# VectorE's operations on neighbouring PSUM banks joined, and a new order of the weights' turning, the scores and the first products of the MLP in a one-core attention and MLP chain

## The chip, the cores and the metric

The kernel runs on one core of a Trainium2 chip. The metric is the time of one execution on the device in microseconds (us). TensorE multiplies matrices and writes the results into PSUM, a memory of eight banks of 128 rows by 512 fp32 columns. VectorE and ScalarE read PSUM; GpSimd works on SBUF alone; SyncE starts DMAs.

## The reference

The input `x` has 4 sequences of 512 tokens with 128 features. Four blocks follow each other, each added to `x` behind a layer norm: attention a (16 heads of width 8), a transformer of two layers (called `ffn`), a linear attention b, and the same `ffn` again. Cut to one `ffn` layer, which is what the change touches:

```python
h = shift_token(x)                       # half of the features come from the token before
q, k, v = split(h @ wqkv)                # 8 heads of width 64
q, k = l2norm(q) * qs, l2norm(k) * ksc
q, k = rotary_xpos(q, k)                 # q * cos * scale + rotate_half(q) * sin * scale
o = local_attention(q, k, v)             # windows of 64 tokens, each sees itself and the one before
x = x + o @ wo
h = layernorm(shift_token(x)) * lg + lb
a, g = split(h @ w1 + b1)
x = x + (a * gelu(g)) @ w2 + b2
```

## The kernel before, in words

`attention_a` (from line 263) does attention a. `stream` then does all the rest as one pipeline. Its unit is a tile of 128 tokens: 2 calls x 2 layers x 4 sequences x 4 tiles = 64 tiles, and four tiles of a sequence are a group (16 groups). The pipeline goes in steps. In step s each engine runs through its list in the table `STEP`; an entry (stage, lag, whose) works on tile s - lag, and group stages (`w1`, `w2`, `wo`, the norms) come every fourth step, stages of attention b (`latent`, `keys_b`, `context`, `tokens_b`, `features_b`, `project_b`) only behind the four groups that end the first call. No scheduler reorders anything: each engine takes its own list in order and waits on semaphores.

A tile k goes this way. TensorE projects q, k and v (L1140 to L1142, three products each, since the numbers are split in a high and a low part). ScalarE squares q and k (L1351) and copies v. VectorE multiplies q and k by the cosine table (L1504) and by the sine table with the halves swapped (L1508), four operations, and sums the squares (L1515). GpSimd adds (L1069) and scales (L1074). A step later TensorE turns q and k (transposes, L1150), ScalarE copies them out (L1371, L1375), TensorE writes the mask into two banks and adds the scores (L1163, L1178), VectorE takes the maxima per bank (L1540) and ScalarE the exponentials (stage `soften`, L1385, eight operations into `PW`). Another step later TensorE turns the weights in two halves (`turn_p` and `turn_p_2`, L1188). ScalarE copies the first half and VectorE the second (L1407, L1532). TensorE sums the values (stage `sums`, L1199) and VectorE divides (L1547, L1551). Then the output is turned (`turn_o`, L1211). Per group follow `wo` (L1238), the centre and the variance of the norm (L1256, L1262), `w1` (L1269: gate and up products of three blocks of the hidden width), the gelu on ScalarE (L1447, between two loads of activation tables, L1442 and L1450), `hidden` on VectorE (L1587) and `w2` (L1277).

A step is named here by the group stage that it holds; they follow each other as `wo`, centre and variance, `w1`, `w2`.

**PSUM.** All results go through the eight banks in rotation. The list `order` in `stream` notes them in TensorE's order, and a result at place x uses bank x mod 8. Before TensorE writes it, `take` waits for the semaphore that frees the last result in this bank (table `FREED`):

```python
def bank(kind, i):
    return at[kind, i] % BANKS
...
"scores": ("exped", lambda i: i + 1), "turn_p": (("p_copied", "p_copied_2"), lambda i: i // 2 + 1),
```

So a place in the order decides not only when TensorE does something but also for whose bank it waits.

Of the kernel before, what the change touches and what calls it, by code (L numbers as in the profile page):

```python
# [10 lines left out]
ACT = mybir.ActivationFunctionType  # L11
ALU = mybir.AluOpType
# [42 lines left out]
def constants():  # L55
# [25 lines left out]
    for name, table in (("cos", cos), ("sin", sin)):  # L81
# [44 lines left out]
def build(nc, a, out):  # L126
    with ExitStack() as top:
# [51 lines left out]
        def scales_tables_and_weights_b():  # L179
# [11 lines left out]
            for layer in range(LAYERS):  # L191
                for i, name in enumerate(("L0_ffn_q_scale", "L0_ffn_k_scale")):
                    v = a[name][layer:layer + 1]
                    at = DW * i
                    pieces.append((g.qks[:, 0, layer, at:at + DW], v.to_broadcast([P, DW])))
                    for half in range(2):
                        dst, src = at + 32 * half, 32 * (1 - half)
                        pieces.append((g.qks[:, 1, layer, dst:dst + 32], v[:, src:src + 32].to_broadcast([P, 32])))
# [4 lines left out]
        with ExitStack() as early:  # L203
            g.tables = sb("tables", [P, 2 * ROPE], ctx=early)

            g.qks = sb("qks", [P, 2, LAYERS, 2 * DW], ctx=early)
            attention_a(nc, a, g)
# [55 lines left out]
def attention_a(nc, a, g):  # L263
# [59 lines left out]
    with ExitStack() as ctx:  # L323
# [38 lines left out]
        with block:  # L362
# [41 lines left out]
            def _(pool):  # L404
# [15 lines left out]
                for work, n in plan:  # L420
# [27 lines left out]
                    elif work == "project" and n == 1:  # L448
                        pool.wait_ge(s("weights"), 16 * len(g.scales_tables_and_weights_b()))
                        for i, table in enumerate((g.cos, g.sin)):  # L450
                            for layer in range(LAYERS):
# [3 lines left out]
                                    g.qks[:, i, layer, None, :].to_broadcast([P, TILES, 2 * DW]), ALU.mult)\  # L455
# [385 lines left out]
def of_first(k):  # L841
# [8 lines left out]
           ("turn_o", 3, of_tile), ("w1", 5, of_group), ("turn_p", 2, of_tile),  # L850
# [3 lines left out]
           ("var_y", 10, of_sequence), ("turn_p_2", 2, of_tile), ("w2", 6, of_group), ("wo", 3, of_group), ("sums", 2, of_tile), ("store", 6, of_end)],  # L854
    "ACT": [("features_a", 0, of_first), ("latent", 8, of_sequence), ("features_b", 10, of_sequence),
            ("squares", 0, of_tile), ("turn", 1, of_tile), ("values", 0, of_tile), ("turn_o", 3, of_tile),
            ("center_mlp", 4, of_group), ("center_a", 2, of_first), ("center_b", 7, of_sequence),
            ("center_y", 10, of_sequence), ("split", SEQS, of_tile), ("w1", 5, of_group), ("turn_p", 2, of_tile), ("keys_b", 8, of_sequence),
            ("norm", 0, of_tile), ("var_mlp", 4, of_group), ("var_a", 2, of_first), ("var_b", 7, of_sequence),
            ("var_y", 10, of_sequence), ("soften", 1, of_tile), ("store", 6, of_end)],  # L860
    "DVE": [("lead", 0, of_lead), ("project_a", 1, of_first), ("latent", 8, of_sequence), ("rope", 0, of_tile), ("context", 9, of_sequence), ("project_b", 10, of_sequence),
            ("w1", 5, of_group), ("keys_b", 8, of_sequence), ("soften", 1, of_tile), ("turn_p_2", 2, of_tile),
            ("tokens_b", 9, of_sequence), ("var_mlp", 4, of_group), ("var_a", 2, of_first),
            ("var_b", 7, of_sequence), ("var_y", 10, of_sequence), ("w1_last", 5, of_group), ("wo", 3, of_group),
# [25 lines left out]
def stream(nc, a, g, out):  # L890
# [4 lines left out]
    order = []  # L895
    for stage, i in engine_plan("PE"):
        if stage == "project":
            order += [("q", i), ("k", i), ("v", i)]
        elif stage == "turn":
            order += [("turned_q", i), ("turned_k", i)]  # L900
        elif stage in ("scores", "sums", "keys_b", "tokens_b"):
            order += [(stage, 2 * i), (stage, 2 * i + 1)]
        elif stage in ("turn_p", "turn_p_2"):
            order += [("turn_p", 2 * i + (stage == "turn_p_2"))]
# [10 lines left out]
    at = {x: i for i, x in enumerate(order)}  # L915

    def bank(kind, i):
        return at[kind, i] % BANKS


    FREED = {"q": ("sin_done", lambda i: 2 * i + 1), "k": ("sin_done", lambda i: 2 * i + 2),
             "v": ("v_copied", lambda i: i + 1),
             "turned_q": ("qk_copied", lambda i: 2 * i + 1), "turned_k": ("qk_copied", lambda i: 2 * i + 2),
             "scores": ("exped", lambda i: i + 1), "turn_p": (("p_copied", "p_copied_2"), lambda i: i // 2 + 1),
             "sums": ("divided", lambda i: i + 1), "turn_o": ("o_copied", lambda i: i + 1),
# [17 lines left out]
    with ExitStack() as ctx:  # L943
# [19 lines left out]
        QT = sb("QT", [P, 2, PAIRS, P])  # L963

        KT = sb("KT", [P, PAIRS, 2 * TILES, WIN])
# [54 lines left out]
        with block:  # L1020
            @block.sync
            def _(sp):
# [4 lines left out]
                for stage, k in engine_plan("SP"):  # L1027
                    if stage == "values":

                        sp.wait_ge(s("v_copied"), k + 1)  # L1030
                        if k >= 4:
                            sp.wait_ge(s("sums"), 2 * k - 6)
# [15 lines left out]
            def _(pool):  # L1048
# [16 lines left out]
                for stage, i in engine_plan("POOL"):  # L1065
                    if stage == "scale":
                        k = i
                        pool.wait_ge(s("sin_done"), 2 * k + 2)
# [44 lines left out]
            def _(pe):  # L1113
                def take(kind, i):
                    x = at[kind, i]
                    if x >= BANKS:
                        earlier, j = order[x - BANKS]
# [36 lines left out]
                def scores(k):  # L1154
# [12 lines left out]
                    pe.wait_ge(s("qk_copied"), 2 * k + 2)  # L1167
                    if k == 0:
                        pe.wait_ge(s("zeroed"), 3)
                    for c in range(PAIRS):  # L1170
                        for w in range(2):
                            for j in range(2):
                                rows = slice(DW * j, DW * j + DW)
                                if t == 0 and w == 0:
                                    keys = KT[rows, c, ::1 - 2 * TILES, :]
                                else:
# [3 lines left out]
                                    QT[rows, k % 2, c, WIN * w:WIN * w + WIN], keys,  # L1180
# [3 lines left out]
                def turn_p(u):  # L1184
                    pe.wait_ge(s("exped"), u + 1)
                    dst = take("turn_p", u)
                    for c in range(PAIRS):
                        last = nc.tensor.transpose(dst[:, P * c:P * c + P], PW[:, u % 4, c, :], g.ident)  # L1188
                    last.then_inc(s("turned_p"), 1)

                def sums(k):
                    pe.wait_ge(s(f"moved{k % 4}"), moved(k))
                    for j in range(2):
# [8 lines left out]
                        last.then_inc(s("sums"), 1)  # L1202

                def turn_o(k):

                    dst = take("turn_o", k).rearrange("p (cc j q) -> p cc j q", cc=2, j=2)
                    for j in range(2):
                        u = 2 * k + j
                        pe.wait_ge(s("divided"), u + 1)
# [6 lines left out]
                for stage, i in engine_plan("PE"):  # L1216
# [6 lines left out]
                    elif stage == "turn_p":  # L1223
                        turn_p(2 * i)
                    elif stage == "turn_p_2":
                        turn_p(2 * i + 1)
# [115 lines left out]
            def _(act):  # L1342
                nc.scalar.preload_act_table_set(EXP_AND_LN)
                for stage, i in engine_plan("ACT"):
# [8 lines left out]
                    elif stage == "values":  # L1353
# [4 lines left out]
                        if k >= 4:  # L1358
                            act.wait_ge(s("sums"), 2 * (k - 3))

                            act.wait_ge(s(f"moved{(k - 3) % 4}"), moved(k - 3))
# [3 lines left out]
                    elif stage == "turn":  # L1365
                        k = i
                        t = k % TILES
                        act.wait_ge(s("turned"), 2 * k + 1)
                        if k >= 2:
                            act.wait_ge(s("scores"), k - 1)  # L1370
                        nc.scalar.activation(QT[:, k % 2, :, :],  # L1371
                                             psum[:, bank("turned_q", k), :].rearrange("p (c x) -> p c x", c=PAIRS),
                                             ACT.Copy).then_inc(s("qk_copied"), 1)
                        act.wait_ge(s("turned"), 2 * k + 2)
                        nc.scalar.activation(KT[:, :, 2 * t:2 * t + 2, :],  # L1375
                                             psum[:, bank("turned_k", k), :].rearrange("p (c s x) -> p c s x",
                                                                                       c=PAIRS, s=2),
                                             ACT.Copy).then_inc(s("qk_copied"), 1)
                    elif stage == "soften":
                        for u in (2 * i, 2 * i + 1):  # L1380
                            act.wait_ge(s("maxed"), u + 1)
                            if u >= 4:
                                act.wait_ge(s("turned_p"), u - 3)
# [4 lines left out]
                            last.then_inc(s("exped"), 1)  # L1388
# [13 lines left out]
                    elif stage == "turn_p":  # L1402
                        u = 2 * i
                        act.wait_ge(s("turned_p"), u + 1)
                        if u >= 4:
                            act.wait_ge(s("sums"), u - 3)
# [81 lines left out]
            def _(dve):  # L1488
# [6 lines left out]
                for stage, i in engine_plan("DVE"):  # L1495
                    if stage == "rope":
                        k = i
                        layer, n, t = place(k)
                        if k >= 2:
                            dve.wait_ge(s("turned"), 2 * k - 2)  # L1500
                        for w, kind in enumerate("qk"):
                            dve.wait_ge(s("squared"), 2 * k + w + 1)
                            x = psum[:, bank(kind, k), :]
                            nc.vector.tensor_tensor(  # L1504
                                A[:, k % 2, w, :].rearrange("p (h d) -> p h d", d=DW),
                                x.rearrange("p (h d) -> p h d", d=DW),
                                g.cos[:, layer, t, w, None, :].to_broadcast([P, HW, DW]), ALU.mult)
                            nc.vector.tensor_tensor(  # L1508
                                BS[:, k % 2, w, :].rearrange("p (h s d) -> p h s d", s=2, d=DW // 2),
                                x.rearrange("p (h s d) -> p h s d", s=2, d=DW // 2)[:, :, ::-1, :],  # L1510
                                g.sin[:, layer, t, w, :].rearrange("p (s d) -> p s d", s=2)[:, None, :, :]
                                 .to_broadcast([P, HW, 2, DW // 2]), ALU.mult).then_inc(s("sin_done"), 1)
# [14 lines left out]
                    elif stage == "turn_p_2":  # L1527
                        u = 2 * i + 1
                        dve.wait_ge(s("turned_p"), u + 1)
                        if u >= 4:  # L1530
                            dve.wait_ge(s("sums"), u - 3)
# [3 lines left out]
                    elif stage == "soften":  # L1535
                        dve.wait_ge(s("scores"), i + 1)
                        for u in (2 * i, 2 * i + 1):
                            if u >= 4:
                                dve.wait_ge(s("exped"), u - 3)
                            nc.vector.tensor_reduce(  # L1540
                                NM[:, u % 4, :], psum[:, bank("scores", u), :].rearrange("p (c x) -> p c x", c=PAIRS),
# [146 lines left out]
```

## Time and profile before

| | us |
|---|---|
| median of 3 runs | 1045.31 (1042.32 to 1049.79) |
| the profiled execution | 1047.65 |
| its span, first to last instruction | 1045.7 |
| busy: TensorE, VectorE, ScalarE, GpSimd | 966.4, 734.2, 740.3, 387.6 |

The stream takes the span from about 280 us on. Busy time of TensorE is counted from modelled ends, so the distance from one block's start to the next block's start is the better measure of what a block costs. A number in brackets behind a row is the idle time of the engine before it and what ended it.

### The profile page before, as it was taken

The numbers are of one execution on the slowest core, as the hardware profiler recorded it, in microseconds if no ns is written. First come the engines' busy times: TensorE is split into PE (matmuls) and PEld (weight loads), VectorE is DVE, ScalarE is ACT, GpSimd is POOL, SyncE is SP. The second block draws the span as 40 slices with busy tenths as digits, with TensorE's granted clock in tenths as the row PEclk, the third lists the DMA queues.
The fourth block names the chain that finished last, engine by engine and source line by source line (L and its number), as shares of the span: only waits on it lengthen the run. The fifth ranks groups of instructions, "written<-read, shape, count | busy, mean of one in ns | idle before, by whom it ended". The sixth has DMA issues, their size and how long they took to land.

```text
span 1045.7 us, 22953 instructions
## 1 busy us (share of the span) xinstructions
PE 966.4 (92%) x8720; PEld 590.2 (56%) x8720; DVE 734.2 (70%) x1218; ACT 740.3 (71%) x1568; POOL 387.6 (37%) x270
## 2 busy tenths in 40 slices
PE   5899999999789999999998898989899999999985
PEld 2333333333466666666666666656566666666752
DVE  3787777776586777777776676767677777776751
ACT  3377777667587877878868575767668778788762
POOL 3010113000466555364543443424264553635410
PEclk9999999989899999999999998999999999999999
DMA  2200000000231010010100000000001100111100
GB/s 68 66 15 1 2 2 2 2 2 2 61 73 27 22 27 22 17 32 17 28 22 17 22 16 12 22 16 22 7 22 27 27 22 17 32 27 27 32 17 15
DMA packets 25223, 23.73 MB, mean 23 GB/s; under 512 B 10610, under 2 KB 17052, under 8 KB 25116
## 3 DMA queue, kind: packets, MB, share of 16 engines
q1 hardware_dynamic: 25116, 22.27, 9.1%
q8 instruction: 71, 1.16, 0.5%
q14 instruction: 36, 0.29, 0.1%
HBM read 6.16 MB, written 1.05 MB: 7 GB/s over the span
## 4 chain that ended last, share of the span: by engine, by line
PE 62%; DVE 7%; issue 2%; ACT 2%; POOL 2%; DVEq 0%; POOLq 0%
PE psum L1269 8%; PE psum L1238 5%; PE psum L1178 5%; PE psum L1199 5%; PE psum L1150 5%; PE psum L1140 5%; PE psum L1188 4%; PE psum L1141 4%; PE psum L1142 4%; PE psum L1277 4%; PE psum L1262 3%; PE psum L1211 2%; PE psum L1256 2%; PE psum L1163 2%; DVE f_PT L1532 2%
## 5 line engine op out<-in xcount | busy, mean ns | idle before, releaser
L1069 POOL TENSOR_TENSOR f_A<-f_A,f_BS 128x1024 f32<-128x1024 f32 x64 | 151.0, 2360 | 222.1 <-DVE f_BS L1508 221.8
L745 DVE TENSOR_REDUCE a_M<-psum 128x2 f32<-128x1024 f32 x128 | 154.0, 1220 | 44.5 <-PE psum L549 43.9
L677 ACT ACTIVATE a_PT<-psum 128x1024 f32<-128x1024 f32 x128 | 130.4, 1023 | 46.0 <-PE psum L559 45.3
L1074 POOL TENSOR_TENSOR f_A<-f_A,f_RN 128x1024 f32<-128x1024 f32 x64 | 121.8, 1903 | 90.7 <-ACT f_RN L1400 86.8
L1385 ACT ACTIVATE f_PW<-psum,f_NM 128x128 f32<-128x128 f32 x512 | 138.4, 380 | 4.2 <-DVE f_NM L1540 4.2
L1540 DVE TENSOR_REDUCE f_NM<-psum 128x4 f32<-128x512 f32 x128 | 82.3, 685 | 66.3 <-PE psum L1178 65.2
L1351 ACT ACTIVATE f_SQ<-psum 128x512 f32<-128x512 f32 x128 | 75.3, 608 | 71.0 <-PE psum L1142 66.4
L1504 DVE TENSOR_TENSOR f_A<-psum,cos 128x512 f32<-128x512 f32 x128 | 87.8, 686 | 44.5 <-ACT f_SQ L1351 44.4
L1199 PE MATMUL psum<-f_VS,f_PT 128*64 128x65 f32 x1024 | 81.2, 228 | 32.5 <-DVE f_hidden L1587 13.8
L1199 PEld LDWEIGHTS psum<-f_VS,f_PT 128*64 128x64 f32 x1024 | 67.8, 139 | 65.5 <-issue 48.3
L1269 PE MATMUL psum<-f_mid,f_w 128*128 128x512 f32 (+1 forms) x192 | 86.8, 603 | 2.7 <-DVE f_mid L1570 2.7
L1508 DVE TENSOR_TENSOR f_BS<-psum,sin 128x512 f32<-128x512 f32 x128 | 87.2, 681 | 0.0
L486 PE MATMUL psum<-a_PT,a_VA 128*12 128x256 f32 x1024 | 82.2, 395 | 0.1
L1199 PE MATMUL psum<-f_V,f_PT 128*64 128x65 f32 x1024 | 81.5, 228 | 0.0
L1188 PE MATMUL psum<-const,f_PW 128*128 128x128 f32 x512 | 78.8, 277 | 0.0
L1515 DVE TENSOR_REDUCE f_SS<-f_SQ 128x16 f32<-128x1024 f32 x64 | 77.4, 1209 | 0.0
L1188 PEld LDWEIGHTS psum<-const,f_PW 128*128 128x128 f32 x512 | 59.3, 141 | 27.8 <-issue 27.8
L1150 PE MATMUL psum<-const,f_A 128*128 128x128 f32 x512 | 66.6, 273 | 6.0 <-POOL f_A L1074 6.0
L1150 PEld LDWEIGHTS psum<-const,f_A 128*128 128x128 f32 x512 | 59.6, 141 | 16.3 <-POOL f_A L1074 7.8
L1178 PE MATMUL psum<-f_KT,f_QT 64*64 64x128 f32 x2048 | 67.7, 271 | 0.1
L1199 PEld LDWEIGHTS psum<-f_V,f_PT 128*64 128x64 f32 x1024 | 67.8, 139 | 0.0
L1178 PEld LDWEIGHTS psum<-f_KT,f_QT 64*64 64x64 f32 x2048 | 60.9, 134 | 5.1 <-ACT f_KT L1375 0.6
(191 smaller groups left out, 1948.8 us busy)
## 6 DMA issues: line engine op xcount, KB each, us to landing
f_VS<-f_V SPq DMA_DIRECT2D x112, 130.0 KB, 2.3
raw<-L_ffn_wqkv_dram SPq DMA_DIRECT2D x2, 768.0 KB, 5.6
a_XT<-L_attn_a_x_dram SPq DMA_DIRECT2D x4, 256.0 KB, 2.9
a_QS<-a_MROW SPq DMA_DIRECT2D x64, 2.0 KB, 1.8
out_dram<-f_OUT SPq DMA_DIRECT2D x4, 256.0 KB, 2.3
f_w<-L_ffn_w_dram SPq DMA_DIRECT2D x2, 341.0 KB
tables<-const_dram SPq DMA_DIRECT2D x1, 512.0 KB, 3.9
f_wo<-L_ffn_wo_dram SPq DMA_DIRECT2D x8, 64.0 KB
```

The costliest lines, as they stand in the source:

```text
L677: nc.scalar.activation(PT[:, i % 4, :, :], psum[:, pair("by_key", i), :], ACT.Exp, scale=float(DA) ** -0.5).then_inc(s("exped"), 1)
L745: nc.vector.tensor_reduce(M[:, quads % 2, t, 2 * j:2 * j + 2], psum[:, pair("scores", i), :], AX_X, ALU.max).then_inc(s("maxed"), 1)
L1069: nc.gpsimd.tensor_tensor(A[:, k % 2, :, :], A[:, k % 2, :, :], BS[:, k % 2, :, :], ALU.add)\
L1074: nc.gpsimd.tensor_tensor(x, x, RN[:, k % 2, :, None].to_broadcast([P, 2 * HW, DW]), ALU.mult)\
L1150: last = nc.tensor.transpose(dst[:, P * c:P * c + P], A[:, k % 2, w, P * c:P * c + P], g.ident)
L1178: last = nc.tensor.matmul(dst[j][WIN * w:WIN * w + WIN, P * c:P * c + P].rearrange("p (s x) -> p s x", s=2), QT[rows, k % 2, c, WIN * w:WI ...
L1188: last = nc.tensor.transpose(dst[:, P * c:P * c + P], PW[:, u % 4, c, :], g.ident)
L1199: last = nc.tensor.matmul(dst[WIN * w:WIN * w + WIN, c, :], PT[:, u % 4, c, WIN * w:WIN * w + WIN], values[:, k % 4, 2 * c + j, :], start= ...
L1269: nc.tensor.matmul(take(kind, 3 * i + blk)[0:w, :], w1[:, layer, first + lo:first + lo + w], mid[:, :], start=True, stop=True).then_inc(s( ...
L1385: last = nc.scalar.activation(PW[:, u % 4, c, :], psum[:, bank("scores", u), P * c:P * c + P], ACT.Exp, bias=NM[:, u % 4, c:c + 1])
L1504: nc.vector.tensor_tensor(A[:, k % 2, w, :].rearrange("p (h d) -> p h d", d=DW), x.rearrange("p (h d) -> p h d", d=DW), g.cos[:, layer, t, ...
L1508: nc.vector.tensor_tensor(BS[:, k % 2, w, :].rearrange("p (h s d) -> p h s d", s=2, d=DW // 2), x.rearrange("p (h s d) -> p h s d", s=2, d ...
```

## The change

It does three things.

First, q and k, the two banks of scores, of sums, of turned q and k, and of the turned weights, are put in neighbouring banks (`together`, which leaves a place empty where a pair would break over the last bank). VectorE then does one operation over both banks where it did two: the cosine and sine products, the maxima, the reciprocals, the divisions. The sine table is stored with its halves swapped, and the halves of the result are swapped on writing. ScalarE copies turned q and k in one operation, and q now lives in extra places of the tile `KT`. The semaphores count pairs: `roped` (one per tile) in place of `sin_done` (two), and `exped`, `divided`, `sums`, `qk_copied` once per tile.

Second, on TensorE both halves of the weights are turned in one stage, ahead of the turned output and of the scores.

Third, `w1` stands behind the scores and the variance on TensorE, and behind them on ScalarE and VectorE too; all of `hidden` is done in one stage.

```diff
     "PE": [("features_a", 0, of_first), ("project_a", 1, of_first), ("latent", 8, of_sequence),
...
-           ("turn_o", 3, of_tile), ("w1", 5, of_group), ("turn_p", 2, of_tile),
+           ("turn_p", 2, of_tile), ("turn_o", 3, of_tile),
...
-           ("var_y", 10, of_sequence), ("turn_p_2", 2, of_tile), ("w2", 6, of_group), ("wo", 3, of_group), ("sums", 2, of_tile), ("store", 6, of_end)],
+           ("var_y", 10, of_sequence), ("w1", 5, of_group), ("w2", 6, of_group), ("wo", 3, of_group), ("sums", 2, of_tile),
...
+    def together(first, second):
+
+        if len(order) % BANKS == BANKS - 1:
+            order.append(None)
+        order.extend((first, second))
...
-    FREED = {"q": ("sin_done", lambda i: 2 * i + 1), "k": ("sin_done", lambda i: 2 * i + 2),
+    FREED = {"q": ("roped", lambda i: i + 1), "k": ("roped", lambda i: i + 1),
...
-             "scores": ("exped", lambda i: i + 1), "turn_p": (("p_copied", "p_copied_2"), lambda i: i // 2 + 1),
-             "sums": ("divided", lambda i: i + 1), "turn_o": ("o_copied", lambda i: i + 1),
+             "scores": ("exped", lambda i: i // 2 + 1), "turn_p": (("p_copied", "p_copied_2"), lambda i: i // 2 + 1),
+             "sums": ("divided", lambda i: i // 2 + 1), "turn_o": ("o_copied", lambda i: i + 1),
...
+                        dve.wait_ge(s("squared"), 2 * k + 2)
                         if k >= 2:
                             dve.wait_ge(s("turned"), 2 * k - 2)
-                        for w, kind in enumerate("qk"):
-                            dve.wait_ge(s("squared"), 2 * k + w + 1)
-                            x = psum[:, bank(kind, k), :]
...
+                        x = two_banks(("q", k), ("k", k))
+                        nc.vector.tensor_tensor(
+                            A[:, k % 2, :, :].rearrange("p w (h d) -> p w h d", d=DW),
+                            x.rearrange("p w (h d) -> p w h d", d=DW),
+                            g.cos[:, layer, t, :, None, :].to_broadcast([P, 2, HW, DW]), ALU.mult)
+                        nc.vector.tensor_tensor(
+                            BS[:, k % 2, :, :].rearrange("p w (h s d) -> p w h s d", s=2, d=DW // 2)[:, :, :, ::-1, :],
...
-                            last.then_inc(s("exped"), 1)
+                        last.then_inc(s("exped"), 1)
```

On TensorE, the `w1` step of one group. Before, from the turned q and k to the first value sum (L1150 turns q and k, L1211 the output, L1269 is `w1`, L1188 the two halves of the weights, L1163 and L1178 masks and scores, L1199 the sums):

```order
L1150 MATMUL psum<-const,f_A 128x128 x8
L1211 MATMUL psum<-const,f_ON 128x128 x4
L1269 MATMUL psum<-f_mid,f_w 128x512 x4
L1269 MATMUL psum<-f_mid,f_w 85x512 x2
L1188 MATMUL psum<-const,f_PW 128x128 x4
L1163 MATMUL psum<-constb 64x512 x4
L1178 MATMUL psum<-f_KT,f_QT 64x128 x16
L1188 MATMUL psum<-const,f_PW 128x128 x4
```

In the changed kernel, the same stretch from the turned output (L1224) on, with the semaphores waited for; L1175 and L1190 are masks and scores, L1280 is `w1`, L1212 the sums:

```order
L1224 MATMUL psum<-const,f_ON 128x128 x4
L1175 MATMUL psum<-constb 64x512 [waits f_roped]
L1175 MATMUL psum<-constb 64x512 x3
L1190 MATMUL psum<-f_KT 64x128 [waits f_qk_copied]
L1190 MATMUL psum<-f_KT 64x128 x15
L1280 MATMUL psum<-f_mid,f_w 128x512 [waits f_v_copied,f_ln_done]
L1280 MATMUL psum<-f_mid,f_w 128x512 [waits f_qk_copied] x2
L1280 MATMUL psum<-f_mid,f_w 128x512 [waits f_p_copied]
L1280 MATMUL psum<-f_mid,f_w 85x512 [waits f_p_copied_2]
L1280 MATMUL psum<-f_mid,f_w 85x512 [waits f_o_copied]
L1212 MATMUL psum<-f_VS,f_PT 64x65 [waits f_exped,f_p_copied,f_moved2]
```

The scores moved from behind `w1` to ahead of it, the second half of the weights from behind the scores to ahead of them, and the sums directly behind `w1`.

On ScalarE, the same step. Before, from the copy of the turned output (L1416) to the exponentials (L1385):

```order
L1416 ACTIVATE f_OT<-psum 128x4x128
L1442 ACT_TABLE_LOAD
L1447 ACTIVATE f_gates<-psum,f_b 128x512 x2
L1447 ACTIVATE f_gates<-psum,f_b 85x512
L1450 ACT_TABLE_LOAD
L1407 ACTIVATE f_PT<-psum 128x512
L1392 ACTIVATE f_LN<-f_SS,tiny 128x16
L1395 ACTIVATE f_LN<-f_LN,tiny 128x16
L1400 ACTIVATE f_RN<-f_LN 128x16
L1385 ACTIVATE f_PW<-psum,f_NM 128x128 x8
```

In the changed kernel (L1427 is the copy of the turned output, L1458 the gelu, L1396 the exponentials):

```order
L1427 ACTIVATE f_OT<-psum 128x4x128
L1403 ACTIVATE f_LN<-f_SS,tiny 128x16
L1406 ACTIVATE f_LN<-f_LN,tiny 128x16
L1411 ACTIVATE f_RN<-f_LN 128x16
L1453 ACT_TABLE_LOAD
L1458 ACTIVATE f_gates<-psum,f_b 128x512 x2
L1458 ACTIVATE f_gates<-psum,f_b 85x512
L1461 ACT_TABLE_LOAD
L1396 ACTIVATE f_PW<-psum,f_NM 128x128 x8
```

The copy of the weights' first half (L1407) and the norm's three small operations now come ahead of the gelus, and the exponentials come straight behind the second table load.

## Rows read from the trace of the kernel before

**Rows 1.** The page: engine, busy us, share of the span, instructions.

```profile
PE 966.4 (92%) x8720; PEld 590.2 (56%) x8720; DVE 734.2 (70%) x1218; ACT 740.3 (71%) x1568; POOL 387.6 (37%) x270
```

**Rows 2.** The waits: engine, line, waited for, us in total, times, longest us.

```profile
PE psum L1199 <- DVE f_hidden L1587: 13.8, 4, 3.5
PE psum L1199 <- DVE f_PT L1532: 13.4, 26, 1.1
...
PE psum L1199 <- DVE f_mid L1566: 5.1, 4, 1.3
```

**Rows 3.** The timeline of TensorE, four steps: start us, us, engine, line, operation.

```profile
491.54 0.50 PE L1140 MATMUL psum<-f_qkv_h,HH 128*128 128x512 f32 x1
...
501.90 0.50 PE L1140 MATMUL psum<-f_qkv_h,HH 128*128 128x512 f32 x1
...
504.10 1.04 PE L1150 MATMUL psum<-const,f_A 128*128 128x128 f32 x8
504.97 0.60 PE L1211 MATMUL psum<-const,f_ON 128*128 128x128 f32 x4
505.41 0.60 PE L1188 MATMUL psum<-const,f_PW 128*128 128x128 f32 x4
505.85 1.02 PE L1256 MATMUL psum<-f_mid,const 128*128 128x512 f32 x2
506.80 0.41 PE L1163 MATMUL psum<-constb 64*64 64x512 bf16 x4
...
508.01 1.12 PE L1262 MATMUL psum<-f_ln_squared,const 128*128 128x512 f32 x2
...
510.98 0.50 PE L1140 MATMUL psum<-f_qkv_h,HH 128*128 128x512 f32 x1
...
514.49 5.32 PE L1269 MATMUL psum<-f_mid,f_w 128*128 128x512 f32 x12
519.64 0.60 PE L1188 MATMUL psum<-const,f_PW 128*128 128x128 f32 x4
...
524.09 0.51 PE L1140 MATMUL psum<-f_qkv_h,HH 128*128 128x512 f32 x1
...
528.13 0.41 PE L1163 MATMUL psum<-constb 64*64 64x512 bf16 x4
...
533.59 0.49 PE L1140 MATMUL psum<-f_qkv_h,HH 128*128 128x512 f32 x1
```

**Rows 4.** The timeline of ScalarE in the same steps.

```profile
502.90 1.30 ACT L1351 ACTIVATE f_SQ<-psum 128x512 f32<-128x512 f32 x2 [2.40 <-PE psum L1142]
...
509.18 0.69 ACT L1436 ACTIVATE f_LR<-psum,eps 128x512 f32<-128x512 f32 x1 [0.40 <-PE psum L1262]
509.90 0.63 ACT L1439 ACTIVATE f_LR<-f_LR 128x512 f32<-128x512 f32 x1
510.43 2.16 ACT L1385 ACTIVATE f_PW<-psum,f_NM 128x128 f32<-128x128 f32 x8
...
518.98 0.68 ACT L1447 ACTIVATE f_gates<-psum,f_b 85x512 f32<-85x512 f32 x1 [0.53 <-PE psum L1269]
519.68 1.28 ACT L1450 ACT_TABLE_LOAD   x1
520.98 0.60 ACT L1407 ACTIVATE f_PT<-psum 128x512 f32<-128x512 f32 x1
```

**Rows 5.** The timeline of VectorE, first and last of the rope's four products in one step.

```profile
503.60 0.69 DVE L1504 TENSOR_TENSOR f_A<-psum,cos 128x512 f32<-128x512 f32 x1 [0.86 <-ACT f_SQ L1351]
...
505.40 0.68 DVE L1508 TENSOR_TENSOR f_BS<-psum,sin 128x512 f32<-128x512 f32 x1
```

**Rows 6.** The page's costliest groups: a reduction over two banks in the first attention.

```profile
L745 DVE TENSOR_REDUCE a_M<-psum 128x2 f32<-128x1024 f32 x128 | 154.0, 1220 | 44.5 <-PE psum L549 43.9
```

**Rows 7.** Two windows, at and behind a wait for `hidden` (busy of PE, PEld, DVE, ACT, POOL; then the granted clock).

```profile
573.20:576.70 3.50, 0.09 (x4) 0.00 (x0) 3.35 (x10) 1.87 (x8) 0.79 (x1) 1.00 0.00 0
576.70:580.10 3.40, 3.36 (x24) 2.98 (x25) 1.03 (x3) 0.60 (x1) 0.00 (x0) 0.51 0.01 2
```

More of the change, by code:

```diff
@@ L80, in constants @@
     sin = sin * np.where(np.arange(DW) < DW // 2, -1, 1)[None, :]
-    for name, table in (("cos", cos), ("sin", sin)):
+    turned = np.concatenate([np.arange(DW // 2, DW), np.arange(DW // 2)])
+    for name, table in (("cos", cos), ("sin", sin[:, turned])):
         both = np.stack([table * scale * np.float32(QK_SCALE), table / scale], 1)
@@ L194, in scales_tables_and_weights_b @@
                     at = DW * i
[L195 to L198, printed above, removed]
+                    pieces.append((g.qks[:, layer, at:at + DW], v.to_broadcast([P, DW])))
             return pieces
@@ L861 @@
[L861 to L864, printed above, removed]
+            ("var_y", 10, of_sequence), ("w1", 5, of_group), ("soften", 1, of_tile), ("store", 6, of_end)],
@@ L895, in stream @@
     order = []
+    def together(first, second):
+        if len(order) % BANKS == BANKS - 1:
+            order.append(None)
+        order.extend((first, second))
     for stage, i in engine_plan("PE"):
         if stage == "project":
-            order += [("q", i), ("k", i), ("v", i)]
+            together(("q", i), ("k", i))
+            order += [("v", i)]
         elif stage == "turn":
[L900 to L904, printed above, removed]
+            together(("turned_q", i), ("turned_k", i))
+        elif stage in ("scores", "sums", "keys_b", "tokens_b", "turn_p"):
+            together((stage, 2 * i), (stage, 2 * i + 1))
         elif stage == "w1":
@@ L962, in stream @@
         BS = sb("BS", [P, 2, 2, T])
[L963 to L965 removed]
+        KT = sb("KT", [P, PAIRS, 2 * TILES + 4, WIN])
         V = sb("V", [P, 4, HW, DW + 1])
@@ L1115, in take @@
                     x = at[kind, i]
-                    if x >= BANKS:
-                        earlier, j = order[x - BANKS]
+                    before = [y for y in order[x % BANKS:x:BANKS] if y is not None]
+                    if before:
+                        earlier, j = before[-1]
                         name, value = FREED[earlier]
@@ L1179, in scores, with turn_p @@
                                     dst[j][WIN * w:WIN * w + WIN, P * c:P * c + P].rearrange("p (s x) -> p s x", s=2),
-                                    QT[rows, k % 2, c, WIN * w:WIN * w + WIN], keys,
+                                    KT[rows, c, 2 * TILES + 2 * (k % 2) + w, :], keys,
                                     start=False, stop=(c == PAIRS - 1), skip_group_check=True)
                     last.then_inc(s("scores"), 1)
[L1184 to L1189, printed above, removed]
+                def turn_p(k):
+                    pe.wait_ge(s("exped"), k + 1)
+                    for u in (2 * k, 2 * k + 1):
+                        dst = take("turn_p", u)
+                        for c in range(PAIRS):
+                            last = nc.tensor.transpose(dst[:, P * c:P * c + P], PW[:, u % 4, c, :], g.ident)
+                        last.then_inc(s("turned_p"), 1)
                 def sums(k):
@@ L1358, in _ @@
                         if k >= 4:
-                            act.wait_ge(s("sums"), 2 * (k - 3))
+                            act.wait_ge(s("sums"), k - 3)
                             act.wait_ge(s(f"moved{(k - 3) % 4}"), moved(k - 3))
```

124 lines of the change are left out of this document (63 added, 61 removed).

## The prediction

> **What bounds the kernel now.** Read the page first: TensorE is busy 92% of the span [rows 1]. Then the list of waits, of what is left in the stream: ahead of the value sums (L1199) TensorE stands idle for VectorE's `hidden` (4 times, 13.8 us), its copy of the turned weights (26 times, 13.4 us) and `mid` (4 times, 5.1 us) [rows 2]. Then the timeline of TensorE over one group of four steps [rows 3]. A step starts with L1140 (call that time T). The four took 10.36 us (491.54 to 501.90; it holds `wo`), 9.08 (centre and variance), 13.11 (`w1`), 9.50 (`w2`): 42.05 in all. The blocks stand nearly end to end: projections 2.20 (501.90 to 504.10), turning q and k 0.87, turning the output 0.44, half the weights 0.44, centre 0.95, masks and scores 1.21, `w1` 5.15 (514.49 to 519.64), and, by the distances left over, some 1.08 for the sums. So TensorE bounds, and what VectorE or ScalarE saves is worth nothing unless TensorE waits for it. The question is which waits the new order makes.
>
> **The change part by part.**
>
> *VectorE's joined operations.* In a chain, two 512-column products start 0.60 us apart (first at 503.60, fourth at 505.40) and the last takes 0.68 [rows 5]. No row shows a 1024-column product from PSUM; a 1024-column reduction from it takes 1.22 [rows 6], and two unjoined cost 1.28 at most. I take 1.13 from start to start and 1.22 for the last (the 0.60 and 0.68 with 0.53 for 512 more columns; bounds 1.13 and 1.37). The rope's four operations then last 1.13 + 1.22 = 2.35 instead of 506.08 - 503.60 = 2.48. That is 0.13 us. Maxima, divisions and the joined q/k copy save as little each, all of it on engines that TensorE did not wait for most of the time. By themselves I count them at nothing (bounds -0.1 and 0 us per step).
>
> *What joining does to the releases.* The rope now starts only when both squares are done: these start at T+1.00 and last 1.30 [rows 4], so it starts at T+2.35 (before T+1.70) and gives both banks back at T+4.70, seen by TensorE at about T+4.75. Before, q's bank came back at about T+3.0 and k's at T+4.2. Who takes them? With eight banks in rotation, in the new order the scores take the banks of q and k, or of k and v, of the same step, in every step; in nearly half the steps the turned output takes q's. The new order reaches the turned output at T + 2.20 + 0.87 + 0.88 (both halves of the weights) = T+3.95 and the scores at T+4.39. So the scores begin at T+4.75, or at 4.75 + 0.44 = T+5.19 where the turned output waits itself; on average about T+4.9. The joined q/k copy (k turned at about T+3.3, 1.0 us more) ends at T+4.35 and hides behind that and the masks.
>
> In the `w2` step the scores stood at T+4.04 (528.13 - 524.09) [rows 3], and in the `wo` step the same blocks stand ahead of them. They come 0.85 later, and the second half of the weights (some 0.47) no longer stands behind them: +0.38 each, so 10.7 and 9.9 us. In the variance step the centre product waits as well: 4.75 + 0.26 + 0.95 + 1.21 + 0.97 + 1.08 = 9.2 (before 9.08, with some 0.4 of wait for the weights' copy that now goes).
>
> *The `w1` step, first half.* Up to now 5.15 us of `w1` stood ahead of the scores and hid everything. Now they stand bare. The step before ends late on ScalarE: variance (logarithm to exponential's end 509.18 to 510.53, so 1.35), then eight exponentials of 2.16 [rows 4]. The variance goes out at T+7.2 (4.75 + 0.26 + 0.95 + 1.21); the logarithm starts 1.17 later (509.18 - 508.01), the exponentials start as it all ends, at about T+9.6, and end at T+11.7, which is 2.5 us after the next T at 9.2. The squares start at T+2.4, end at T+3.5, the rope at T+5.9; scores at T+5.96 against 4.39, and up to 6.4 with the turned output waiting: end of the scores T+7.2 to 7.6.
>
> *The `w1` step, second half.* This carries the sum. ScalarE's order is now table load, three gelus, table load, exponentials (the last order fence above). The sums of the same step take the banks of the scores of the same step, since `w1` uses six banks in between (2 + 6 = 8), and those are free only when all eight exponentials are done: `waits f_exped` in the second order fence. The third gelu started 518.98 - 514.49 = 4.49 after `w1` did, then 0.70 to the table load, 1.30 to its end, 2.16 of exponentials, 0.10 to TensorE [rows 4]: 8.75 us, against 5.15 of products. TensorE waits 3.6 us. Before, the exponentials followed the same load, but the sums took the banks of the middle `w1` products. Step: 7.4 + 8.75 + 1.08 = 17.2, before 13.11.
>
> One rule would make this worse. The row shows the table load taking 1.28 us (519.68), and the copy behind it starts at 520.98, with no further gap [rows 4]. The Trainium skill (ScalarE: Activation LUTs, What ACT_TABLE_LOAD costs) puts a switch at about 2.66 us, the load and a drain of 1.38. By that the wait would be 5.0 us and the sum 21 us more; the trace disagrees, and I go by its row.
>
> *A group.* 10.7 + 9.2 + 17.2 + 9.9 = 47.0 against 42.05: +4.95. Of 16 `w1` steps the last has no scores or sums. Four others hold the second attention's `context` and `tokens_b`. That leaves 11 ordinary: 11 x 4.95 = +54.5.
>
> *The four with the second attention.* There TensorE already lost 3.45 us each to `hidden` and 1.3 to `mid` [rows 2]. The first falls away as `w1` is now behind, and 3.6 take its place; the second falls away as the copy precedes `mid` on VectorE as before but the joined operations leave it more room; `context` and `tokens_b` fill the new wait ahead of the scores. That is -1.15, with small change -1.5 each and -6 in all (bounds -4 and +1 each: all small waits gone, or the 1.3 kept and the rope's waits added).
>
> *The clock.* In the 3.50 us in which TensorE stood still for one of those waits it was granted 1.00, and in the next 3.40 us 0.51, the 1.2 GHz level [rows 7]; this came behind each of the four. In those 3.4 us it does 1.7 us less work. The new waits are nearly as long (3.6 less the tail of the last product), so I expect the fall behind three in four of the 11: 8 x 1.6 = +13 (bounds 0 and, with a fall behind all and some twice as long, +30).
>
> *The rest.* The tables need 8 fewer small DMAs at the start, hidden behind the first attention: 0. GpSimd adds and scales as before, half a microsecond later in steps that are no shorter: 0, and up to 0.5 a step if it had no room.
>
> *Sum.* +54.5 - 6 + 13 = +61.5 on the profiled execution's 1047.65 us gives 1109; it stands 2.3 above the median of the runs, 1045.31, so by the median 1107. I say 1105, since the stretch at the start has fewer full steps.
>
> **Rivals.** About 1% (10 us) either way is what a measurement here can tell from no change.
>
> A. *Only the wait for the exponentials is new; not slower.* Place: the bank release by the joined rope. If it reaches TensorE by T+4.0 (a rope of 1.6 us in place of 2.35), the scores never wait. A group is then its bare blocks, about 40.0 us (42.05 less some 2.1 of waits), plus 3.6: +1.5, and 11 x 1.5 = +17; the four others lose 3.45, 1.3 and a slow stretch worth 1.6 each, against 3.6: -11. Without clock falls 1045 + 6 = 1051. It decides from 0.4 us of release time. For it: the waits of now are real [rows 2]. Against: two 1024-column reads of PSUM can't be that short [rows 5, 6]. 0.14.
>
> B. *The clock doesn't fall.* The wait is a little shorter than 3.45 us: 1105 - 13 = 1092. For it: only spells of that full length are shown to bring it down [rows 7]. 0.20.
>
> C. *The clock falls behind every wait and twice where the next wait follows:* 1105 + 17 = 1122. The waits for the rope come within the slow stretch. The upper end of the range, 1126, leaves room for some waits for the rope above my 0.85. 0.15.
>
> D. *The change doesn't do what it says for half its places:* the rope wait is half as long as I say, since squares and rope overlap with the step before: half of 11 x 3.5 (4.95 + the 2.1 of old waits, less 3.6) is 19 less, and clock falls at half: 1080. 0.10.
>
> Mine, 1095 to 1118: 0.41.
>
> **How the numbers follow.** Likeliest 1105. The range reaches over B and D's lower side, to 1060, and over C to 1126: left out are A and a little above, about 0.18. Slower by over 1% (above 1056): mine, B, C, D and 0.02 of A: 0.88. The rest of A: 0.08 within 1%, 0.04 faster.
>
> **What would show it.** In the new profile: the sums' first product (L1212) idle for ScalarE's exponentials about 15 times, 3.4 us each, some 50 us; the scores' masks, the centre or the turned output idle for the joined sine product in most steps, 0.3 to 1.5 us each; VectorE busy 30 to 50 us less; joined products at 1.2 us; granted clock at half in a stretch behind most `w1` steps; waits for `hidden` and for the weights' copy gone. I am wrong if the sums follow `w1` with less than 2 us of idle time, if the joined rope takes over 2.8 us (then more is lost in each step), or if the steps between are under 9.5 and 10.4 us.

## The result and the profile after

| | before | after |
|---|---|---|
| median of the runs, us | 1045.47 | 1140.63 (1130.67 to 1143.52, 4 runs) |
| profiled span, us | 1045.7 | 1136.6 |
| mean granted clock of TensorE | 0.980 | 0.958 |

The ratio is 1.089 (95% interval 1.085 to 1.094): slower by 95 us, where I forecast 60. The measured time lies above my range.

The page of the changed kernel, busy time per engine:

```profile
PE 994.6 (88%) x8720; PEld 607.8 (53%) x8720; DVE 708.7 (62%) x898; ACT 745.8 (66%) x1504; POOL 387.6 (34%) x270
```

VectorE does 320 instructions fewer and is busy 25.5 us less [rows 1]; I had said 30 to 50. TensorE does the same number of products and needs 28 us more for them by the modelled ends, most of it at the slow clock (below). The waits of TensorE (who, for whom, us in total, times, longest), in place of [rows 2]:

```profile
PE psum L1212 <- ACT f_PW L1396: 52.5, 15, 3.5
...
PE psum L1175 <- DVE f_BS L1518: 9.4, 16, 1.0
PE psum L1224 <- DVE f_BS L1518: 9.3, 14, 1.3
...
PE psum L1267 <- DVE f_BS L1518: 7.3, 17, 1.1
```

The first is the wait of the sums for the exponentials, 15 times 3.50 us. The other three are masks, turned output and centre waiting for the rope's second joined product, 26.0 us in all. The waits for `hidden` and for the weights' copy are gone.

One group on TensorE, to be laid beside [rows 3]:

```profile
482.10 0.49 PE L1152 MATMUL psum<-f_qkv_h,HH 128*128 128x512 f32 x1
...
491.64 0.50 PE L1152 MATMUL psum<-f_qkv_h,HH 128*128 128x512 f32 x1
...
497.50 0.66 PE L1224 MATMUL psum<-const,f_ON 128*128 128x128 f32 x4 [0.66 <-DVE f_BS L1518]
498.09 0.41 PE L1175 MATMUL psum<-constb 64*64 64x512 bf16 x4
...
499.30 5.42 PE L1280 MATMUL psum<-f_mid,f_w 128*128 128x512 f32 x12
...
508.22 0.34 PE L1212 MATMUL psum<-f_VS,f_PT 128*64 128x65 f32 x1 [3.50 <-ACT f_PW L1396]
...
510.15 0.80 PE L1152 MATMUL psum<-f_qkv_h,HH 128*128 128x512 f32 x1
...
512.97 1.03 PE L1162 MATMUL psum<-const,f_A 128*128 128x128 f32 x8
...
520.68 0.50 PE L1152 MATMUL psum<-f_qkv_h,HH 128*128 128x512 f32 x1
...
531.93 0.50 PE L1152 MATMUL psum<-f_qkv_h,HH 128*128 128x512 f32 x1
```

The steps last 9.54 (variance), 18.51 (`w1`), 10.53 (`w2`) and 11.25 (`wo`): 49.83 against 42.05. (It is the longer of two kinds that take turns: the four steps before these, from 432.94 to 482.10, last 49.16.) From `w1` to the sums it is 8.92 us (8.75 in the prediction). ScalarE in that stretch shows why:

```profile
503.90 0.68 ACT L1458 ACTIVATE f_gates<-psum,f_b 85x512 f32<-85x512 f32 x1 [1.03 <-PE psum L1280]
504.60 1.28 ACT L1461 ACT_TABLE_LOAD   x1
505.90 2.18 ACT L1396 ACTIVATE f_PW<-psum,f_NM 128x128 f32<-128x128 f32 x8
```

Gelu, load, exponentials, end to end until 508.08; the sums start 0.14 later. And the windows at and behind the wait (TensorE's busy time first, its granted clock the fourth number from the end):

```profile
504.70:508.10 3.40, 0.02 (x1) 0.00 (x0) 0.75 (x1) 3.36 (x9) 0.00 (x0) 1.00 0.00 0
508.10:511.50 3.40, 3.28 (x35) 3.01 (x36) 0.90 (x2) 0.00 (x0) 0.00 (x0) 0.50 0.00 0
```

The joined products took what was expected of them (VectorE, one step):

```profile
495.09 1.22 DVE L1514 TENSOR_TENSOR f_A<-psum,cos 128x1024 f32<-128x1024 f32 x1 [0.93 <-ACT f_SQ L1362]
496.23 1.22 DVE L1518 TENSOR_TENSOR f_BS<-psum,sin 128x1024 f32<-128x1024 f32 x1
```

1.14 from start to start and 1.22 for the last.

### The profile page after: what moved, and what is told of

It is laid out like the page before. It is cut to its first block and busy times, and to the rows that moved or that the text cites. A ratio compares the mean times of both kernels' runs of the same rounds, so it can differ in the third digit from the quotient of the medians.

```text
span 1136.6 us, 22373 instructions
## 1 busy us (share of the span) xinstructions
PE 994.6 (88%) x8720; PEld 607.8 (53%) x8720; DVE 708.7 (62%) x898; ACT 745.8 (66%) x1504; POOL 387.6 (34%) x270
## 5 line engine op out<-in xcount | busy, mean ns | idle before, releaser
L1396 ACT ACTIVATE f_PW<-psum,f_NM 128x128 f32<-128x128 f32 x512 | 138.9, 382 | 21.5 <-DVE f_NM L1552 21.3
L1514 DVE TENSOR_TENSOR f_A<-psum,cos 128x1024 f32<-128x1024 f32 x64 | 78.4, 1224 | 87.8 <-ACT f_SQ L1362 87.5
L1212 PE MATMUL psum<-f_VS,f_PT 128*64 128x65 f32 x1024 | 83.0, 241 | 54.2 <-ACT f_PW L1396 52.5
L1212 PEld LDWEIGHTS psum<-f_VS,f_PT 128*64 128x64 f32 x1024 | 73.8, 153 | 102.2 <-issue 102.2
L1552 DVE TENSOR_REDUCE f_NM<-psum 128x8 f32<-128x1024 f32 x64 | 78.1, 1220 | 34.6 <-PE psum L1190 34.6
L1280 PE MATMUL psum<-f_mid,f_w 128*128 128x512 f32 (+1 forms) x192 | 89.6, 617 | 2.7 <-DVE f_mid L1582 2.7
L1212 PE MATMUL psum<-f_V,f_PT 128*64 128x65 f32 x1024 | 83.6, 242 | 0.0
L1385 ACT ACTIVATE f_KT<-psum 128x1024 f32<-128x1024 f32 x64 | 66.2, 1035 | 19.6 <-PE psum L1162 19.1
L1518 DVE TENSOR_TENSOR f_BS<-psum,sin 128x1024 f32<-128x1024 f32 x64 | 77.7, 1214 | 0.0
L1212 PEld LDWEIGHTS psum<-f_V,f_PT 128*64 128x64 f32 x1024 | 73.9, 154 | 0.0
L1201 PE MATMUL psum<-const,f_PW 128*128 128x128 f32 x512 | 67.9, 277 | 1.2 <-ACT f_PW L1396 1.2
L1190 PE MATMUL psum<-f_KT 64*64 64x128 f32 x2048 | 68.1, 271 | 0.8 <-ACT f_KT L1385 0.8
L1190 PEld LDWEIGHTS psum<-f_KT 64*64 64x64 f32 x2048 | 61.6, 134 | 5.2 <-ACT f_KT L1385 1.1
```

Of the source, the lines that this page charges most:

```text
L1190: last = nc.tensor.matmul(dst[j][WIN * w:WIN * w + WIN, P * c:P * c + P].rearrange("p (s x) -> p s x", s=2), KT[rows, c, 2 * TILES + 2 * ( ...
L1212: last = nc.tensor.matmul(dst[WIN * w:WIN * w + WIN, c, :], PT[:, u % 4, c, WIN * w:WIN * w + WIN], values[:, k % 4, 2 * c + j, :], start= ...
L1280: nc.tensor.matmul(take(kind, 3 * i + blk)[0:w, :], w1[:, layer, first + lo:first + lo + w], mid[:, :], start=True, stop=True).then_inc(s( ...
L1396: last = nc.scalar.activation(PW[:, u % 4, c, :], psum[:, bank("scores", u), P * c:P * c + P], ACT.Exp, bias=NM[:, u % 4, c:c + 1])
L1518: nc.vector.tensor_tensor(BS[:, k % 2, :, :].rearrange("p w (h s d) -> p w h s d", s=2, d=DW // 2)[:, :, :, ::-1, :], x.rearrange("p w (h ...
```

## The experiments

Two theories stood at first. W: most of the loss is the wait of the `w1` step's sums for the exponentials' bank, with the slow clock behind it. J: most of it is in the joins, which give back banks and tiles in pairs and so later. Four kernels were to tell them apart.

**joins_only.** The changed kernel with the order table of before.

```diff
-           ("turn_p", 2, of_tile), ("turn_o", 3, of_tile),
+           ("turn_o", 3, of_tile), ("w1", 5, of_group), ("turn_p", 2, of_tile),
...
-           ("var_y", 10, of_sequence), ("w1", 5, of_group), ("w2", 6, of_group), ...
+           ("var_y", 10, of_sequence), ("turn_p_2", 2, of_tile), ("w2", 6, of_group), ...
```

> The changed kernel with the order table of before: pairs joined, w1 ahead of the scores, second half of the weights behind them. Theory W (most of the loss is the wait of the w1 step's sums for the exponentials' bank, 15 times 3.76 us, and the slow clock behind it): 1050 to 1060, the few us from the later release by the joined rope in three of four steps. Rival J (the loss is in the joins, which give banks and tiles back in pairs and so later, in every step): above 1100.

Measured: 1086.3 us, 1.035 of before (1.027 to 1.044). It lies between the two bands and in neither. TensorE's waits:

```profile
PE psum L1175 <- DVE f_BS L1520: 18.0, 23, 1.8
PE psum L1212 <- DVE f_hidden L1601: 13.7, 4, 3.5
PE psum L1212 <- DVE f_PT L1544: 12.1, 26, 0.8
```

The two old waits are there as before, and the masks wait for the rope in addition.

**order_only.** The kernel before with the order table of the change, nothing joined.

```diff
-        elif stage in ("turn_p", "turn_p_2"):
-            order += [("turn_p", 2 * i + (stage == "turn_p_2"))]
+        elif stage == "turn_p":
+            order += [("turn_p", 2 * i), ("turn_p", 2 * i + 1)]
```

> The kernel before with the order table of the change and nothing joined. W: 1100 to 1120; the sums still take the scores' banks, but bank by bank, so the first half goes some 1 us earlier and the wait costs about 3.2 us. J: 1045 to 1060.

Measured: 1093.4 us, 1.047 (1.040 to 1.054), below W's band. The sums wait 42.1 us in 30 pieces for the exponentials (half by half), where the joined form waits 52.5. 1.035 x 1.047 = 1.084, so the two parts nearly make up the 1.089: W and J are both half right. The order brings a wait for the rope even where nothing is joined: the masks wait for it 20 times here, 17.9 us in all.

**skip_two_banks.** The change's order word for word; only the rotation of banks skips two places.

```diff
             order += [(kind, 3 * i + blk) for blk in range(3) for kind in ("gate", "up")]
+            order += [None, None]
```

> The changed kernel, order untouched, but two places of the rotation left empty behind w1, so that the w1 step's sums take the banks of w1's first products and not those of the scores. Nothing else differs. W: the 3.76 us ahead of these sums and the slow clock go, some 1.4 us a group comes back in the next step, where the exponentials end later than its squares could start: 1065 to 1085. J: at most 10 us faster than the changed kernel, 1130.

Measured: 1085.6 us, 1.037 (1.030 to 1.044), 55 us faster than the change. The wait of the sums for the exponentials is gone from the list; the waits for the rope are now 16.4, 15.4 and 5.7 us, 37.5 against 26.0. So what cost 55 us was not where `w1` stood, but whose bank the sums behind it got.

**third_table_load.** A dose on the suspected chain.

```diff
+                        nc.scalar.preload_act_table_set(SQRT)
                         nc.scalar.preload_act_table_set(EXP_AND_LN)
```

> The changed kernel with one more load of an activation table (1.28 us) between the gelus and the exponentials. W: it lies on the chain gelu, load, exponentials, sums in 15 steps: 19 us slower, up to 30 if the clock falls longer: 1160 to 1170. J: ScalarE is 66% busy and hides it: 1141 to 1145.

Measured: 1162.8 us, 22 more than the change. The wait:

```profile
PE psum L1212 <- ACT f_PW L1396: 71.8, 15, 4.8
```

71.8 - 52.5 = 19.3 us, which is 15 x 1.28. All of the dose arrives at TensorE, and no more than the loads themselves.

Next came the joins: which of them costs?

**joins_rope_split.** joins_only with the rope in four operations.

```diff
-                        dve.wait_ge(s("squared"), 2 * k + 2)
-                        x = two_banks(("q", k), ("k", k))
+                        for w, kind in enumerate("qk"):
+                            dve.wait_ge(s("squared"), 2 * k + w + 1)
+                            x = psum[:, bank(kind, k), :]
```

> joins_only (1086 us) with the rope's four operations, their own waits and q's and k's own releases put back; all other pairs stay joined. Theory R (of the joins it is the rope's late release that costs, seen as 0.84 us ahead of the scores in the w2 and wo steps): 1050 to 1060. Rival P (pairs of exps, sums and divisions cost as much, by later releases of their tiles and banks): 1070 to 1080.

Measured: 1057.8 us, 1.010 (1.007 to 1.014): 28.5 us less. The wait of the masks for the rope fell from 18.0 to 2.9 us. The rope is the dear join; some 11 us more than before stay, which I did not break down.

**skip_and_rope_split.** The same edit on skip_two_banks.

> skip_two_banks (1085.6 us) with the rope in four operations and q's and k's own releases. Theory R: the waits for the rope ahead of the turned output and the scores shrink by some 0.5 to 0.8 us in each step: 1050 to 1065. Rival P: 1075 to 1085.

Measured: 1050.2 us, 1.006 (1.003 to 1.009): 35 us less.

**order_skip_banks.** The two places left empty in order_only: the order without joins and without the wait.

> order_only (1093 us) with the two places left empty behind w1. Nothing joined. The 2.46 us ahead of the sums and the slow clock behind 12 of 15 of them go: 15 x 2.7 + 12 x 1.5 is 58 us less, and about 15 come back because the exponentials run into the next step. Expected 1045 to 1055. If the order has other costs beside this wait (the scores bare behind the project stage, in every w1 step): 1060 and more.

Measured: 1050.1 us, 1.005 (1.003 to 1.006), as expected, 43 us less than order_only.

**exps_before_gelus.** The other way to end the wait: on ScalarE, in the changed kernel.

```diff
-            ("var_y", 10, of_sequence), ("w1", 5, of_group), ("soften", 1, of_tile), ("store", 6, of_end)],
+            ("var_y", 10, of_sequence), ("soften", 1, of_tile), ("w1", 5, of_group), ("store", 6, of_end)],
```

> The changed kernel with the exponentials ahead of the gelus on ScalarE; TensorE's order and banks are the change's. The sums still wait for the exponentials, but these end 3.6 us behind the scores, under w1's 5.15. If the wait is the order on ScalarE: no idle time ahead of the sums, no slow clock behind, and ScalarE is free some 0.5 us earlier than in skip_two_banks (1085.6): 1070 to 1085. If something else on the way kept the sums: 1120 and more.

Measured: 1071.4 us, 1.023 (1.020 to 1.027): 69 us less than the change, in the band. The sums still take the scores' banks, and they are free by then: no wait for the exponentials is left among TensorE's large ones.

**exps_first_rope_split.** exps_before_gelus with the rope split.

> exps_before_gelus (1071.4 us) with the rope in four operations. If the two causes add up as so far (rope split gave 28 and 35 us): 1036 to 1044, level with or just below the kernel before. If the exponentials' wait had only moved: 1050 and more.

Measured: 1041.9 us, 0.994 (0.991 to 0.997), in the band.

**w1_back_rope_split.** `w1` ahead of the scores again on all engines, halves ahead, rope split.

> The changed kernel with w1 moved back ahead of the scores on all three engines and the rope in four operations; both halves of the weights stay ahead of the scores and all other pairs stay joined. Against joins_rope_split (1057.8) only the halves' place and hidden's differ: the half of the weights that VectorE copied just in time (0.4 and 1.0 us a group) is early now: 15 to 17 us less, 1038 to 1046. If their place does nothing: 1055 to 1060.

Measured: 1052.0 us, 1.004 (1.000 to 1.008). A miss: 6 us less than joins_rope_split, not 15, and its 12 runs lie far apart (1046 to 1062). The 11.7 us in which the sums waited for the weights' copy went, but the masks, now behind both halves, wait 14.6 us for the rope instead of 2.9.

**halves_only.** The kernel before, both halves of the weights ahead of the scores, nothing else (but that all of `hidden` is one stage).

> The kernel before with one thing of the change: both halves of the weights turned ahead of the turned output and the scores; w1 stays ahead of the scores, nothing is joined. The old waits for the weights' copy (0.4 and 1.0 us a group) go, the exponentials keep w1 as cover: 1025 to 1038. If the scores, now 0.44 us later only, meet a new wait of their own: 1045.

Measured: 1040.9 us, 0.994 (0.991 to 0.997). The gain is 5 us, not the 7 to 20 of the band. The 13.4 us of waits for the weights' copy [rows 2] went, and 12.6 us came in which the masks wait for the rope, 20 times.

**order_exps_first.** The last: order_only with the exponentials ahead of the gelus on ScalarE, by the same edit as in exps_before_gelus.

> order_only (1093 us) with the exponentials ahead of the gelus on ScalarE; nothing joined. order_skip_banks stood at 1050 with the exponentials still ending late in the next step; putting them first took 14 us more than skipping banks did with the joins. If that carries over: 1034 to 1042, the same as exps_first_rope_split, whose remaining joins would then be shown to be worth nothing either way. If the joins left in that kernel help: 1045 to 1052.

Measured: 1031.1 us, 0.986 (0.982 to 0.990): faster than both kernels, 3 us below its band, and 11 us below the same kernel with the other joins (1041.9). So these don't help; the kernel with them is behind by about as much as joins_rope_split was. Whether that is the joined operations or the changed rotation of banks (`together` leaves places empty) no run separates.

ScalarE around its `w1` step:

```profile
474.68 2.17 ACT L1386 ACTIVATE f_PW<-psum,f_NM 128x128 f32<-128x128 f32 x8 [0.30 <-DVE f_NM L1541]
476.87 1.28 ACT L1443 ACT_TABLE_LOAD   x1
478.17 1.83 ACT L1448 ACTIVATE f_gates<-psum,f_b 128x512 f32<-128x512 f32 x3
480.02 1.28 ACT L1451 ACT_TABLE_LOAD   x1
481.31 1.10 ACT L1352 ACTIVATE f_SQ<-psum 128x512 f32<-128x512 f32 x2
```

And TensorE in the same stretch:

```profile
473.68 5.42 PE L1270 MATMUL psum<-f_mid,f_w 128*128 128x512 f32 x12
...
480.12 0.50 PE L1142 MATMUL psum<-f_qkv_h,HH 128*128 128x512 f32 x1
```

On TensorE `w1` started at 473.68. The exponentials end 3.17 us later, inside its 5.15, the gelus run without a gap, and ScalarE is free for the next squares at 481.3, 1.2 us after the next step's start at 480.12.

## Why the prediction was wrong, and what in it was right

The failed step is the one on the four groups with the second attention, which I took as 6 us faster and which were 8.6 slower. The clock was mis-sized (13 us put, some 22 found), and the first steps of the stream, for which I even took 2 us off, lost 6. The two waits that I named are real and of the size that I gave. By stretches of the two profiled executions, from the starts of the steps on TensorE:

| stretch | before, us | after, us | difference | forecast |
|---|---|---|---|---|
| up to the stream's first step | 272.9 | 267.35 | -5.5 | 0 |
| steps 0 to 7 | 69.85 | 75.8 | +5.9 | 0 |
| nine ordinary groups, steps 8 to 27 and 44 to 59 | 385.5 | 452.4 | +66.9 | |
| four groups with the second attention, steps 28 to 43 | 228.1 | 236.7 | +8.6 | -6 |
| the last two ordinary groups and the end | 89.3 | 104.3 | +15.0 | |
| all 11 ordinary groups (the nine, and the last two with the end) | 474.9 | 556.8 | +81.9 | +67.5 (54.5 and 13 for the clock) |

**The wait of the sums** (3.6 us, 15 times, said in the `w1` step, second half): right. 3.50 us of idle time each, and the start of the sums 3.77 us late (8.92 less the 5.15 of before). skip_two_banks and exps_before_gelus take it away in two ways and give back 55 and 69 of the 95 us, and third_table_load adds to it: it is the cause of more than half the loss. The larger price of a table load that I set aside (a wait of 5.0 us) doesn't show: the exponentials start 0.02 us behind the load.

**The release by the joined rope**: right in place, and about right in size. Where the masks waited alone they came at T+4.85, against the 4.75 of the prediction:

```profile
372.33 0.51 PE L1152 MATMUL psum<-w_h,HH 128*128 128x512 f32 x1
...
377.18 0.41 PE L1175 MATMUL psum<-constb 64*64 64x512 bf16 x4 [0.29 <-DVE f_BS L1518]
```

The price of the operation was also right (1.14 and 1.22). Splitting the rope gave back 28, 35 and 29 us in three pairs of kernels. In the `wo` step I took the average over the two cases, 4.9; in the group above it was the worse case, 526.01 - 520.68 = 5.33.

**The clock**: this term was mis-sized. I put a fall behind three of four of the 11 waits, 13 us. There is one behind each of the 11; five last 3.4 us and six 6.8. At full speed it is 3.28 us from the start of the sums to the turning of q and k (the 1.08 and 2.20 of the prediction). In the group above it is 512.97 - 508.22 = 4.75, so 1.5 us more. In the next group the fall lasts 6.8 us, and it is 562.98 - 557.23 = 5.75, so 2.5 us more:

```profile
557.23 0.34 PE L1212 MATMUL psum<-f_VS,f_PT 128*64 128x65 f32 x1 [3.50 <-ACT f_PW L1396]
...
562.98 0.49 PE L1162 MATMUL psum<-const,f_A 128*128 128x128 f32 x3
```

The window of this fall, in part still in the wait:

```profile
555.90:562.70 6.80, 5.47 (x40) 4.66 (x41) 0.90 (x2) 2.36 (x7) 0.00 (x0) 0.50 0.01 2
```

Read so, ten of the 11 lost 20 us; with an estimate of 2 for the last, which has no projections behind it, that is 22 us, 9 more than I put. Rival C, with falls behind all and some twice as long, put 30 and ended at 1122. The mean clocks (0.980 and 0.958) would give 27 us, but they aren't a price: they count half speed also where TensorE stood idle, and a fall of the kernel before in the first attention, which the change leaves as it was:

```profile
204.70:218.30 13.60, 13.58 (x72) 4.47 (x71) 7.19 (x9) 6.98 (x8) 0.00 (x0) 0.50 0.01 1
```

That fall is the likely reason why the stream began 5.5 us earlier in the changed kernel. It is luck, and it made the miss look smaller.

**The four groups with the second attention**: this step failed. I took 6 us off, with bounds of -4 and +1 for each. From the step 28 to the step 44 of tiles, before:

```profile
559.64 0.50 PE L1140 MATMUL psum<-f_qkv_h,HH 128*128 128x512 f32 x1
...
787.73 0.50 PE L1140 MATMUL psum<-w_h,HH 128*128 128x512 f32 x1
```

and after:

```profile
598.26 0.50 PE L1152 MATMUL psum<-f_qkv_h,HH 128*128 128x512 f32 x1
...
834.95 0.49 PE L1152 MATMUL psum<-w_h,HH 128*128 128x512 f32 x1
```

228.1 us before, 236.7 after: +8.6. TensorE's waits in this stretch after:

```profile
PE psum L1212 <- ACT f_PW L1396: 14.0, 4, 3.5
PE psum L1267 <- DVE X L1676: 4.5, 4, 1.1
PE psum L1152 <- DVE f_mid L1578: 3.7, 3, 1.2
PE psum L1267 <- DVE f_BS L1518: 3.2, 7, 0.7
PE psum L1321 <- issue: 2.4, 4, 0.6
PE psum L1175 <- DVE f_BS L1518: 0.9, 1, 0.9
```

That is 28.7 us; before it was 18.8: 13.8 for `hidden`, 3.8 for `mid`, 1.0 for `X` and 0.2 for the weights' copy. One for one the sums' wait took the place of `hidden`, as I had said. Three things I had wrong. First, I wrote that the wait for `mid` falls away; it stayed (3.8 us before, 3.7 after). It is for the centre's bank, which `mid` frees only after the variance, and VectorE stood waiting for ScalarE's part of it, so that its room was not the question. Second, `context` and `tokens_b` hid the rope in the `w1` steps, but in the steps between centre and masks wait for it, 4.1 us. Third, waits came that I hadn't looked for: the centre behind the second attention for VectorE's sum `X` (+3.5 us), and the first product of `tokens_b` (L1321, 2.4 us; what it waits for the profile doesn't say). TensorE's own work took 1 us less.

**The ordinary groups** without the clock: 49.83 less 1.5 and 49.16 less 2.5, by turns, is 47.5 on average against my 47.0. That is 5 us in 11 groups; 0.17 of each is the wait of the sums.

**The first eight steps**: I expected less than a full share there and took 2 us off. They lost 6: centre, turned output and masks wait for the rope, up to 1.3 us at a time.

**The rivals.** A is refuted: the rope's wait is real. B too: the clock fell. D (half the rope's waits) is refuted by where the masks stand, T+4.85 and T+5.33. From the stream's first step on 35 us are missing (96.4 against 61.5): 15 in the four groups, 9 for the clock, 6 in the first steps and 5 in the ordinary groups.

## What to carry to other kernels

Where results go through banks in rotation, a new order is also a new list of who waits for whose bank: count the places between a result and the one that takes its bank, and look what its reader has in front of it in its own queue. Skipping two places, or moving eight exponentials ahead of three gelus, was worth 55 and 69 us here, and the same order with the exponentials first (order_exps_first) beats the kernel before by 1.4%. Joining two operations saves their fixed part on an engine that may not be waited for, and gives the first bank back later on one that is: here 25 us less busy on VectorE, and 28 to 35 us lost by the rope's join alone, in three pairs of kernels that differ in it.

## What the runs showed of the hardware

The clock of TensorE fell after shorter idle spells than [rows 7] made me expect. In order_only the sums stood idle for 2.46 us in each of 15 `w1` steps, and a stretch at half followed 12 of them, as here:

```profile
363.40:366.20 2.80, 0.38 (x13) 0.41 (x15) 0.74 (x1) 2.79 (x8) 0.00 (x0) 1.00 0.00 0
366.30:369.70 3.40, 3.10 (x27) 2.54 (x24) 1.21 (x4) 0.51 (x3) 0.00 (x0) 0.50 0.00 0
```

1.2 GHz for the next 3.4 us. In the changed kernel an idle spell of 3.50 us came 15 times: 8 times a fall of 3.4 us went with it, 6 times one of 6.8 us, and once, in step 28, none.

Where the clock fell, an idle TensorE thus cost its own 3.50 us and 1.5 or 2.5 us more in the work behind it.
